# One pipeline over groups of four node tiles in place of three stages: joining the carried rows, the first layer norm and the gate of the experts

## What is computed

```python
xn = _layernorm(x)
x = x + _L0_gnn_ref(xn, src, dst, ...) + _L0_mix_ref(xn, ...)   # segment_max(relu(...)) per node, plus a linear-attention mixer
x = x + _L0_ffn_ref(_layernorm(x), Wr, br, W1, ..., Wo, bo)
xn = _layernorm(x)
x = x + _L1_gnn_ref(xn, edge_index, ...) + _L1_mix_ref(xn, ...)  # three SAGE convolutions: segment mean, two products
x = x + _L1_ffn_ref(_layernorm(x), ...)                          # top half of the nodes through an MLP

def _L0_ffn_ref(x, Wr, br, ...):
    w = softmax(x @ Wr + br)                 # the gate: 3125 x 8
    ...                                      # eight experts: two hidden layers with batch norm, then Wo
    return einsum('bfed,fe->bfd', y, w)
```

## Time and profile before

| | |
|---|---|
| median of 3 executions | 2261.87 us (2258.31 to 2263.03) |
| the profiled execution | 2258.0 us |
| its span (first to last instruction) | 2256.2 us |
| PE busy | 1725.8 us, 76% |
| DVE busy | 1298.2 us, 58% |
| POOL busy | 1140.9 us, 51% |
| ACT busy | 594.2 us, 26% |

### The profile page before, as it was taken

One profiled execution on the slowest core, in us unless ns is written; L12 is line 12 of the kernel. 1 busy time (PEld: TensorE's weight loads), 2 busy tenths in 40 slices (PEclk: granted clock), 3 DMA queues, 4 the chain that ended last, 5 costly groups with the idle time before them and its releaser, 6 DMA issues. The chain is left out here.

```text
span 2256.2 us, 25614 instructions
## 1 busy us (share of the span) xinstructions
PE 1725.8 (76%) x8399; PEld 1001.1 (44%) x8399; DVE 1298.2 (58%) x2568; ACT 594.2 (26%) x937; POOL 1140.9 (51%) x888
## 2 busy tenths in 40 slices
PE   7984644545543638999999259799989999997996
PEld 6862222212222414555555138655565555544543
DVE  6868857676775635777777144645541221125996
ACT  4001101111111215666666131311220010003453
POOL 0868888888886777888888857200000000000444
PEclk9557876868776868999999667799999999997998
DMA  6346888888868202111111020244325533421002
GB/s 173 84 134 196 223 213 217 222 222 217 232 190 196 46 3 55 35 34 34 34 34 13 1 67 2 49 106 109 99 51 130 127 92 97 123 79 38 1 6 80
DMA packets 193170, 229.06 MB, mean 102 GB/s; under 512 B 66574, under 2 KB 174178, under 8 KB 187697
## 3 DMA queue, kind: packets, MB, share of 16 engines
q1 hardware_dynamic: 125887, 172.58, 28.7%
q0 software_dynamic: 67200, 55.46, 11.1%
HBM read 148.81 MB, written 78.24 MB: 101 GB/s over the span
## 5 line engine op out<-in xcount | busy, mean ns | idle before, releaser
L709 POOL DMA_INDIRECT adjacency<-all_cell_val,all_cell_idx x400 | 543.4, 1358 | 151.3 <-issue 120.4
L275 POOL DMA_INDIRECT edge_ring<-b_rows,all_src_idx x400 | 494.3, 1236 | 187.6 <-issue 170.8
L1662 POOL TENSOR_TENSOR ffn_hl<-ffn_hid,ffn_hh 128x448 f16<-128x448 f32 x56 | 70.1, 1254 | 727.2 <-ACT ffn_hid L1679 727.1
L1475 PE MATMUL bank<-sage_adj,sage_zh 125*128 125x448 f16 x1050 | 370.1, 352 | 3.4 <-DVE sage_zl L1529 3.4
L1475 PE MATMUL bank<-sage_adj,sage_zl 125*128 125x448 f16 x1050 | 370.0, 352 | 0.0
L529 DVE SCALAR_TENSOR_TENSOR edge_ring<-edge_ring,w_keep 125x256 f32<-125x256 f32 x399 | 192.9, 484 | 122.8 <-DMA edge_ring<-b_rows,all_src_idx 105.9
L1552 DVE TENSOR_TENSOR sage_u<-bank,w_rd 128x448 f32<-128x448 f32 x42 | 26.2, 624 | 236.8 <-PE bank L1480 234.0
L1475 PEld LDWEIGHTS bank<-sage_adj,sage_zh 125*128 125x128 f16 x1050 | 102.6, 98 | 101.8 <-issue 8.0
L1475 PEld LDWEIGHTS bank<-sage_adj,sage_zl 125*128 125x128 f16 x1050 | 102.7, 98 | 99.6 <-issue 5.8
L684 DVE SCALAR_TENSOR_TENSOR edge_junk<-bank,all_key_c,all_later 125x400 f16<-125x400 f32 x232 | 145.5, 627 | 0.0
L823 PE MATMUL bank<-all_a,w_W1h 128*128 (+1 forms) x448 | 123.4, 358 | 25.0 <-ACTq L1118 25.0
(11 more groups left out here) (424 smaller groups left out, 3576.8 us busy)
## 6 DMA issues: line engine op xcount, KB each, us to landing
sage_adj<-adjacency SPq DMA_DIRECT2D x105, 490.0 KB
run_max<-edge_ring SPq DMA_DIRECT2D x40, 1120.0 KB
adjacency<-edge_zero SPq DMA_DIRECT2D x25, 714.0 KB
experts_gb<-gate_rows SPq DMA_DIRECT2D x56, 224.0 KB, 3.2
edge_ring<-b_rows,all_src_idx POOLq DMA_INDIRECT x400, 6.8
adjacency<-all_cell_val,all_cell_idx POOLq DMA_INDIRECT x400, 2.7
sage_adj<-adjacency SPq DMA_DIRECT2D x105, 56.9 KB
run_max<-edge_ring SPq DMA_DIRECT2D x40, 130.0 KB
```

Of the source, the lines that this page charges most:

```text
L275: nc.gpsimd.indirect_dma_start(ring[:, k % RING, :], None, dram.rows[:, :], bass.IndirectOffsetOnAxis(ap=c.src_idx[:, k:k + 1], axis=0)).t ...
L709: nc.gpsimd.indirect_dma_start(dram.adj_flat, bass.IndirectOffsetOnAxis(ap=c.cell_idx[:, k:k + 1], axis=0), c.cell_val[:, k:k + 1], None). ...
L1475: ins = mm(ps[4 * b + h][:, 0:T], z[:, g * JG + j, half(h)], adj[g][:, j, :], start=(g == 0 and j == 0 and z is zh), stop=False)
L1662: nc.gpsimd.tensor_tensor(hl[:, m, :], hid[:, m, :], hh[:, m, :], ALU.subtract).then_inc(low, 1)
```

## The change

join_max, norm 1 and gate become one stage, join_norm_gate (L866 of the changed file), with one barrier. It works in steps t = 0 to 9: in step t the engines take group t's masks and transposes, the join adds and the mean of group t-1, the centring, square and variance of group t-2, and the reciprocal, scale, halves and logits of group t-3. norm stays for its other two uses.

- The carried rows' numbers (carry_rows, the same plane as before) are loaded by SP in the edge stage behind its 37th of 40 batches, and hot is a tile of its own.
- m is a ring of MR = 8 tiles. From the ninth gather on POOL first places one cell, then waits until the group that had the buffer is transposed (turned), then gathers. 29 cells follow.
- The variance is a product of the 1/256 matrix with the squares, 128x500 in PSUM; root and reciprocal work on 128x500 in PSUM, and nothing is transposed.
- The logits have y as weights and Wr as eight moving columns, and come out with nodes on partitions; the bias is a row spread over 125 partitions. ACT and DVE share the last copies.
- The experts read the halves from c.eh and c.el, which lie in c.yn's plane.
- Weight pieces: ACT writes a high half in each step from t = 2, DVE a low half in each step from t = 3; Wo is loaded over W1's buffer, two blocks for each W1 piece done.
- Cells: 46 in the new stage, 229 in the experts, 47 in norm 2, 78 in mix1.

The diff, cut to its core (new file's DVE and PE programs in full; "..." where lines are left out):

```diff
+JOINED = 46
...
+                        if n == NBAT - 4:
+                            sp.wait_ge(side_stored, 64)
+                            sp.wait_ge(mixed, (NT - 1) * DVE_N + 5)
+                            sp.dma_start(c.carry_rows, dram.carry.partition_broadcast(NONE + 1)).then_inc(rows_in, 16)
...
-                sp.wait_ge(side_stored, 64)
+                sp.wait_ge(rows_in, 16)
...
+def join_norm_gate(nc, c, dram, w, loads, plan):
+    MR = 8
+    mats, first, second = loads
...
+        for j in range(NB):
+            if j >= MR:
+                place_cells(nc, c, dram, pool, j - MR, j - MR + 1)
+                pool.wait_ge(turned, 2 * ((j - MR) // 4) + 2)
+            nc.gpsimd.indirect_dma_start(m[:, j % MR, :], None, dram.runs[:, :],
+                                         bass.IndirectOffsetOnAxis(ap=c.last_idx[:, j:j + 1], axis=0)).then_inc(got[j % MR], 16)
+        place_cells(nc, c, dram, pool, NB - MR, JOINED)
...
+        for t in range(2, G4 + 3):
+            g = t - 3
+            if g >= 0:
+                act.wait_ge(var_done, g + 1)
+                if g >= 1:
+                    act.wait_ge(scaled, g)
+                nc.scalar.activation(ps[4][:, 0:wide(g)], ps[3][:, 0:wide(g)], ACT.Sqrt, bias=c.eps5[:, 0:1]).then_inc(sd_ready, 1)
+            highs(t - 2)
+            if g >= 0:
+                act.wait_ge(scaled, g + 1)
+                nc.scalar.copy(c.eh[:, :, at(g)], y[:, g % 2, :, 0:wide(g)]).then_inc(high, 1)
+            g = t - 2
+            if g < G4:
+                act.wait_ge(centred, g + 1)
+                if g >= 1:
+                    act.wait_ge(var_done, g)
+                nc.scalar.activation(sq[:, :, 0:wide(g)], y[:, g % 2, :, 0:wide(g)], ACT.Square).then_inc(sq_ready, 1)
+        act.wait_ge(ready, 1)
+        nc.scalar.activation(lg[:], lg[:], ACT.Exp).then_inc(ex, 1)
+        for n in range(G4 + 1, len(parts)):
+            highs(n)
+        for g in range(1, G4, 2):
+            act.wait_ge(w_turned, g + 1)
+            nc.scalar.copy(hot[0:NEXP, at(g)], ps[g][0:NEXP, 0:wide(g)]).then_inc(w_copied[1], 1)
...
+        def lows(n):
+            src, hi, lo, _, _ = parts[n]
+            dve.wait_ge(split_high, n + 1)
+            v.scalar_tensor_tensor(lo, src, WS, hi, ALU.mult, ALU.subtract).then_inc(split_low, 1)
+        for t in range(G4 + 3):
+            if t < G4:
+                for j in range(4 * t, 4 * t + size(t)):
+                    dve.wait_ge(got[j % MR], 16 * (j // MR + 1))
+                    dve.wait_ge(spread, j + 1)
+                    v.tensor_tensor(m[:, j % MR, :], m[:, j % MR, :], ps[6 + j % 2][0:B, 0:D], ALU.max).then_inc(masked, 1)
+            if t >= 3:
+                g = t - 3
+                dve.wait_ge(sd_ready, g + 1)
+                v.reciprocal(ps[4][:, 0:wide(g)], ps[4][:, 0:wide(g)]).then_inc(rs_ready, 1)
+            if 1 <= t <= G4:
+                g = t - 1
+                for h in range(KH):
+                    dve.wait_ge(turned, 2 * g + h + 1)
+                    step(v.tensor_tensor(t1[:, 0:wide(g)], ps[h][:, 0:wide(g)], c.a[:, h, at(g)], ALU.add))
+                    ins = v.scalar_tensor_tensor(c.xT[:, h, at(g)], t1[:, 0:wide(g)], 0.0, c.xT[:, h, at(g)], ALU.max, ALU.add)
+                    if h == 0:
+                        step(ins)
+                ins.then_inc(joined, 1)
+            if t == 1:
+                fold_bn()
+            if t >= 3:
+                g = t - 3
+                dve.wait_ge(rs_ready, g + 1)
+                for h in range(KH):
+                    ins = v.tensor_tensor(y[:, g % 2, h, 0:wide(g)], y[:, g % 2, h, 0:wide(g)], ps[4][:, 0:wide(g)], ALU.mult)
+                ins.then_inc(scaled, 1)
+            if 2 <= t <= G4 + 1:
+                g = t - 2
+                dve.wait_ge(mean_done, g + 1)
+                if g >= 2:
+                    dve.wait_ge(logits, g - 1)
+                    dve.wait_ge(lowed, g - 1)
+                for h in range(KH):
+                    ins = v.tensor_tensor(y[:, g % 2, h, 0:wide(g)], c.xT[:, h, at(g)], ps[2][:, 0:wide(g)], ALU.subtract)
+                ins.then_inc(centred, 1)
+            if t >= 3:
+                g = t - 3
+                dve.wait_ge(high, g + 1)
+                dve.wait_ge(scaled, g + 1)
+                v.tensor_tensor(c.el[:, :, at(g)], y[:, g % 2, :, 0:wide(g)], c.eh[:, :, at(g)], ALU.subtract).then_inc(lowed, 1)
+            if 3 <= t < G4 + 2:
+                lows(t - 3)
+        dve.wait_ge(br_in, 16)
+        dve.wait_ge(logits, G4)
+        step(v.tensor_tensor(lg[:], ps[5][0:B, 0:NB * NEXP].rearrange("p (j e) -> p j e", e=NEXP),
+                             br[:].unsqueeze(1).to_broadcast([B, NB, NEXP]), ALU.add))
+        wide_mx = mx[:].unsqueeze(2).to_broadcast([B, NB, NEXP])
+        step(v.tensor_reduce(mx[:], lg[:], AX.X, ALU.max))
+        v.tensor_tensor(lg[:], lg[:], wide_mx, ALU.subtract).then_inc(ready, 1)
+        for n in range(G4 - 1, len(parts) - 4):
+            lows(n)
+        dve.wait_ge(ex, 1)
+        step(v.tensor_reduce(mx[:], lg[:], AX.X, ALU.add))
+        step(v.reciprocal(mx[:], mx[:]))
+        v.tensor_tensor(lg[:], lg[:], wide_mx, ALU.mult).then_inc(ready, 1)
+        for g in range(0, G4, 2):
+            dve.wait_ge(w_turned, g + 1)
+            v.tensor_copy(hot[0:NEXP, at(g)], ps[g][0:NEXP, 0:wide(g)]).then_inc(w_copied[0], 1)
+            lows(len(parts) - 4 + g // 2)
...
+        for t in range(G4 + 3):
+            if t + 1 < G4:
+                for j in range(4 * t + 4, 4 * t + 4 + min(2, size(t + 1))):
+                    spread_carry(j)
+            if t < G4:
+                pe.wait_ge(masked, 4 * t + size(t))
+                if t >= 1:
+                    pe.wait_ge(joined, t)
+                for h in range(KH):
+                    for i in range(size(t)):
+                        ins = nc.tensor.transpose(ps[h][:, B * i:B * (i + 1)], m[:, (4 * t + i) % MR, half(h)], c.ident[0:B, 0:B])
+                    ins.then_inc(turned, 1)
+            if t >= 3:
+                g = t - 3
+                pe.wait_ge(scaled, g + 1)
+                for i in range(size(g)):
+                    j = 4 * g + i
+                    ins = product(nc, ps[5][0:B, NEXP * j:NEXP * (j + 1)], [y[:, g % 2, k, B * i:B * (i + 1)] for k in range(KH)],
+                                  [w.Wr[:, k, :] for k in range(KH)])
+                ins.then_inc(logits, 1)
+            if 1 <= t <= G4:
+                g = t - 1
+                pe.wait_ge(joined, g + 1)
+                if g >= 1:
+                    pe.wait_ge(centred, g)
+                product(nc, ps[2][:, 0:wide(g)], [c.mean_w[:]] * KH, [c.xT[:, k, at(g)] for k in range(KH)]).then_inc(mean_done, 1)
+            if 2 <= t <= G4 + 1:
+                g = t - 2
+                pe.wait_ge(sq_ready, g + 1)
+                if g >= 1:
+                    pe.wait_ge(sd_ready, g)
+                product(nc, ps[3][:, 0:wide(g)], [c.mean_w[:]] * KH, [sq[:, k, 0:wide(g)] for k in range(KH)]).then_inc(var_done, 1)
+            if t + 1 < G4:
+                for j in range(4 * t + 6, 4 * t + 4 + size(t + 1)):
+                    spread_carry(j)
+        pe.wait_ge(ready, 2)
+        for g in range(G4):
+            for i in range(size(g)):
+                ins = nc.tensor.transpose(ps[g][0:NEXP, B * i:B * (i + 1)], lg[:, 4 * g + i, :], c.ident[0:B, 0:B])
+            ins.then_inc(w_turned, 1)
...
+                v.memset(out[:, :, N:NP], 0.0)
...
-                                       [(c.yh[:, k, cols(t)], c.yl[:, k, cols(t)]) for k in range(KH)])
+                                       [(c.eh[:, k, cols(t)], c.el[:, k, cols(t)]) for k in range(KH)])
...
-                join_max(nc, c, dram, w, plan, pieces(f[0], w.W1, mats[0]))
-                norm(nc, c, 1, lambda pool: place_cells(nc, c, dram, pool, 8, 40), [(f[0][:, e], blocks(i.Wo)[:, e], mats[2]) for e in each])
-                gate(nc, c, w, dram, pieces(f[1], w.W2, mats[1]) + pieces(f[0], w.Wo, mats[2]), lambda pool: place_cells(nc, c, dram, pool, 40, 64))
+                join_norm_gate(nc, c, dram, w, ([(f[0][:, e], blocks(i.Wo)[:, e], mats[2]) for e in each],
+                                                pieces(f[0], w.W1, mats[0]) + pieces(f[1], w.W2, mats[1]),
+                                                pieces(f[0], w.Wo, mats[2])), plan)
             made = g.sem("cells_made")
-            experts(nc, c, w, dram, made, lambda pool: place_cells(nc, c, dram, pool, 64, 330, made))
+            experts(nc, c, w, dram, made, lambda pool: place_cells(nc, c, dram, pool, JOINED, 275, made))
...
-                norm(nc, c, 2, lambda pool: place_cells(nc, c, dram, pool, 330, 350), [
+                norm(nc, c, 2, lambda pool: place_cells(nc, c, dram, pool, 275, 322), [
-            mix1(nc, c, w, qT, ctx, lambda pool: place_cells(nc, c, dram, pool, 350, L))
+            mix1(nc, c, w, qT, ctx, lambda pool: place_cells(nc, c, dram, pool, 322, L))
```

221 lines of the change are left out of this document (82 added, 139 removed).

## The result

The change makes the kernel slower. Its median is 2280.39 us (2278.80 to 2281.72, four executions) against 2261.82 us before: ratio 1.009, 95% interval 1.0077 to 1.0102, or +18.6 us where +8 was forecast. The profiled execution took 2278.8 us with a span of 2277.2, so 20.8 more than the profiled execution before.

The account below looks back on a forecast made before the run. No early stage had an engine full throughout; POOL's queue plus seams set the end. An earlier experts start, -12.1, and later cells, +20.6, summed to +8.5: 2266.5 profiled, 2270 median; own range 2262 to 2277, 8 in 10 2249 to 2285.

Parts of the forecast that it names:

- rival (c): New stage's pipeline: PE at the low clock throughout, a step of 19.4 us, 2283 us; chance 0.20 together with (d).
- The edge stage and the first masks (1): Carry rows' load moved to the edge stage: costs 0 (bounds 0 to 3); first group masked at 709.6, as before.
- The ring (2): Eight gather buffers at the new stage's start: gather and cell pairs take 3.0 us, group 3's masks end at 738.
- The step (3): One pipeline step: 16.95 us, with PE's logits, mean and variance 7.8 together (bounds 5.5 and 10.2).
- My sign for being right: In the step's window, DVE waits for PE before the reciprocal or masks, with the clock between 0.6 and 0.9.
- The order on PE and the reciprocal: In each step, DVE's reciprocal, 3.3 us, comes behind PE's logits, mean, variance and spreads and the last mask.
- The end of the stage and the store (4): Last scale to gate store: last copy ends at 838.2, experts' first matmul at 842.7 against 854.8, so -12.1 us.
- The cells (5): Experts to SAGE: the experts' tail goes, but norm 2 and mix 1 become POOL-bound, 612.6 against 592.0, +20.6 us.
- Full clock (a): Pipeline: PE stays warm, its middle three parts take 5.5 and not 7.8, 2258 us; chance 0.20.
- DVE-paced (b): Pipeline: DVE sets the step and no engine waits for another, 12.5 us a step, 2247 us; chance 0.12.
- (d): Experts: if cells take more than 1.77 us, POOL ends behind PE again, +5; chance 0.20 together with rival (c).

Follow-up runs that it names:

- E9: The change itself, unaltered, run again on another set's chip against the kernel before: 2279.32 us, ratio 1.0036.
- E8: The change with the carry rows' load moved back from the edge stage into the new stage: 2277.48 us, ratio 1.005 to the kernel before.
- E10: The carry rows' load back in the new stage again, beside the unaltered change on one chip: 2275.92 us, ratio 1.003 to the kernel before.
- E4: The change with no cell between the join's gathers, all 46 behind the last: 2274.63 us, ratio 1.0065 to the kernel before.
- E7: The change with the variance narrow as before, root and reciprocal on 125x4, and four transposes: 2261.94 us, ratio 0.9979 to the kernel before.
- E3: The change with PE's variance and late spreads put ahead of logits and mean in each step: 2262.22 us, ratio 1.0007 to the kernel before.
- E1: The change with 68 cells in the new stage (46) and 56 in mix 1 (78): 2251.25 us, ratio 0.9958 to the kernel before.
- E2: The change with cells divided as in the kernel before (64, 266, 20, 50): 2259.27 us, ratio 0.9995 to the kernel before.
- E12: The change with variance first and narrow, cells 52, 231, 25, 92, no cell between gathers, late carry-row load: 2261.63 us, ratio 0.9953 to the kernel before.

## Why the prediction came out as it did

**The direction and the mechanism were right, the size was under half.** Of the profiled 20.8 us, I had 8.5. The median, 2280.4, lies outside the forecast's own range (2262 to 2277) and inside the wide one only because rival (c) had stretched it. In the set of E9 the same change cost 9.2 us, so how well +8 fits depends on the set, and that is luck.

*The edge stage and the first masks (1).* Zero, as predicted for the time: E8 and E10 put the early load at 0 to 3.4 us of loss, the bounds I gave it. The cover named, the gathers' own landing, is the one that the trace shows.

*The ring (2).* Masks of group 3 were to end at 738; they ended at 738.1. E4 shows that this term, which I had only followed, was worth 5 us.

*The step (3).* This is the term that was mis-sized. It has PE's part as logits 3.0, mean 2.6 and variance 2.2, 7.8 together. Measured in the full steps: 3.37 to 3.53, 3.41 to 3.68, and 1.84 to 3.12. Most of the error is in the mean, which I had put between the two levels and which ran at the low one. The transposes' 1.90 come ahead of them, of which I counted nothing though DVE's scale hides only 1.25. From the end of one scale to the next it was 17.5, 19.0, 17.4, 15.5, 13.3 and 6.5, where I had 17.0, 17.0, 16.0, 14.4, 11.2 and 5.4. That is 8 us up to the last scale, 834.3 against 826.3, and T1 was late by just these 8. The clock was at its low level in most of each burst and rose only toward its end. My sign for being right, a clock of 0.6 to 0.9 in the step's window, came true (0.66) for another reason than I had: it was not the bursts that ran between the levels, it was the pauses that ran high. The rule of the Trainium skill ("TensorE: Matmul & The Clock Gate", section "HAM oscillation — how this bites in real kernels"), that waits between bursts make each next one start cold, describes this trace: PE waits 5.3 to 6.9 us in each step, and each burst begins at the low clock (0.50 in the first 4.9 us of the bursts at 744, 761 and 781). I gave the rival built on it 0.20 and took the middle; the measured T1 (850.7) lies nearer to its 855.4 than to my 842.7. Rival (c) was thus right about logits and mean; it went too far in keeping the variance low as well. What the rule doesn't tell is E7, where PE waited less, was busy 40 of 45 us, and had the lower clock.

*The order on PE and the reciprocal.* The prediction said that the reciprocal waits behind logits and mean; E3 shows it at 16 us of T1 and E7 the reciprocal itself at 15. It priced the order but did not ask for another.

*The end of the stage and the store (4).* Tail 12.1 us from the last scale to the last copy's end, 11.9 predicted; last copy to T1 4.3, predicted 4.5. POOL idle from 811, predicted 808.

*The cells (5).* T1 to norm 2 405.0 (405.6), norm 2's 47 cells 72.9 (71.0), mix 1's 78 cells 121.3 (118.6), T1 to SAGE 614.1 (612.6). E1 and E2 confirm this term: with the old division the loss is gone (0.9995), with 22 cells moved from mix 1 it turns into a gain.

*What was not in it.* 3.0 us behind SAGE's start. In the twelve profiles of E1 to E12 the same stretch took 808.7 to 815.3, and in the second profile of the unaltered change (E9) 809.4, as in the kernel before; so I count it as spread. The medians' +18.6 may have less of it than the profile's 20.8.

**The rivals.** Full clock (a) and DVE-paced (b) did not come; (c) nearly did. (d) did not: the cells beside the experts took 1.73 each (328.39 / 229 + 0.30), and POOL was done 5 us ahead of DVE.

## What to carry to other kernels

When one queue (here POOL with 400 scatters) spans many stages, add up where it will be idle before merging stages around it: a shorter stage gains nothing if its share of the queue's work lands where the queue is last. In a pipeline of several engines, put on each engine first what another one waits for: moving the variance ahead of two other groups of instructions on PE brought T1 forward by 16 us, computing it another way by 15, and the two together by 11. Before merging, try what the old stages give with the queue divided anew: here that took half of the best gain. Take durations of matmul bursts that follow waits from rows at the low clock, and look at the clock of the bursts, not at the mean of a window with pauses in it.
